# Score and maximum matmuls of two softmax attentions reading 64 and 62 rows of a half array in place of 50 and 48

## The reference

```
x = x + L0_xattn(_layernorm(x), ctx)      # softmax attention, 16 heads of 16
x = x + L0_ffn(_layernorm(x))             # top 2 of 8 experts
x = x + L1_xattn(_layernorm(x), ctx, ctx) # autocorrelation by FFT, top 6 lags
x = x + L1_ffn(_layernorm(x))             # top 1 of 4 experts
x = x + L2_xattn(_layernorm(x), ctx, ctx) # sigmoid attention
x = x + L2_ffn(_layernorm(x))             # shared part and top 2 of 8
x = x + L3_xattn(_layernorm(x), ctx)      # softmax attention
x = x + L3_ffn(_layernorm(x))             # top 1 of 16 scale and bias
```

## Time and profile before

| | us |
|---|---|
| runs, median (lowest, highest) | 2725.03 (2724.96, 2748.5) |
| the profiled execution | 2749.48 |
| its span, first to last instruction | 2747.7 |
| around the span (the difference) | 1.8 |
| TensorE / VectorE / ScalarE / GpSimd busy | 2600.0 / 1634.8 / 1573.2 / 326.9 |
| mean granted TensorE clock | 0.942 |

### The profile page before, as it was taken

One profiled execution on the slowest core, in us unless ns is written; L12 is line 12 of the kernel. 1 busy time (PEld: TensorE's weight loads), 2 busy tenths in 40 slices (PEclk: granted clock), 3 DMA queues, 4 the chain that ended last, 5 costly groups with the idle time before them and its releaser, 6 DMA issues.

```text
span 2747.7 us, 46488 instructions
## 1 busy us (share of the span) xinstructions
PE 2600.0 (95%) x18464; PEld 1281.6 (47%) x18464; DVE 1634.8 (59%) x2983; ACT 1573.2 (57%) x2691; POOL 326.9 (12%) x280
## 2 busy tenths in 40 slices
PE   7999999999899779999899999989999999999987
PEld 3334344333377657776233333268633343434433
DVE  6877788778387664442112221057587788878844
ACT  1777777776701112111687978932247777777763
POOL 2010100100003311121010010012201001010001
PEclk7899999998999889999999999989969899999988
DMA  5433334322210001001844646210043342334300
GB/s 120 72 37 38 61 43 67 45 29 25 73 29 16 1 16 54 1 1 36 123 49 73 72 64 75 52 51 1 14 59 60 37 73 36 38 61 48 38 1 31
DMA packets 68636, 125.13 MB, mean 46 GB/s; under 512 B 20979, under 2 KB 45630, under 8 KB 64966
## 3 DMA queue, kind: packets, MB, share of 16 engines
q1 hardware_dynamic: 67270, 119.73, 28.5%
q10 hardware_dynamic: 1152, 2.44, 0.4%
HBM read 41.59 MB, written 2.10 MB: 16 GB/s over the span
## 4 chain that ended last, share of the span: by engine, by line
PE 54%; DVE 4%; ACT 3%; issue 1%; SPq 1%; ACTq 0%; DMA 0%; POOL 0%; POOLq 0%; DVEq 0%
PE psum L202 24%; PE psum L748 13%; PE psum L213 9%; PE psum L2109 6%; ACT probs L816 2%; DVE mpart L938 2%; PE psum L308 1%; PE psum L2102 1%; SPq L1054 1%; DMA qst<-qp_lo 0%; SPq L1055 0%; PE psum L758 0%; ACTq L1054 0%; ACTq L1055 0%; DVE stats L335 0%
## 5 line engine op out<-in xcount | busy, mean ns | idle before, releaser
L816 ACT ACTIVATE probs<-psum 128x512 f32<-128x512 f32 (+3 forms) x2080 | 1266.4, 690 | 311.8 <-PE psum L202 304.0
L938 DVE TENSOR_REDUCE mpart<-psum 128x2 f32<-128x804 f32 x1024 | 972.6, 990 | 265.6 <-PE psum L202 254.6
L748 PE MATMUL psum<-probs,vt 128*17 128x512 f32 (+1 forms) x4992 | 674.1, 619 | 3.6 <-ACT probs L816 2.9
L202 PE MATMUL psum<-qst,kst 50*128 50x512 f32 (+3 forms) x2496 | 624.6, 450 | 18.8 <-ACT probs L816 7.7
L202 PE MATMUL psum<-kst,qst 48*128 48x402 f32 x2048 | 490.1, 426 | 22.4 <-DVE mpart L938 19.6
L202 PEld LDWEIGHTS psum<-qst,kst 50*128 50x128 f32 (+3 forms) x2496 | 294.7, 188 | 393.4 <-issue 212.5
L202 PEld LDWEIGHTS psum<-kst,qst 48*128 48x128 f32 x2048 | 240.5, 200 | 314.4 <-DVE mpart L938 174.6
L748 PEld LDWEIGHTS psum<-probs,vt 128*17 128x17 f32 (+1 forms) x4992 | 92.9, 96 | 218.9 <-issue 181.5
L213 PE MATMUL psum<-wv,ctxT 128*32 128x256 f32 (+1 forms) x2448 | 172.8, 402 | 0.8 <-DVE kp_lo L919 0.8
L213 PE MATMUL psum<-ctxT,wk 128*32 128x512 f32 (+1 forms) x1536 | 147.8, 510 | 11.8 <-DMA ctxT<-in_ctxT 9.4
L2154 ACT ACTIVATE inner<-psum 128x512 f32<-128x512 f32 x32 | 19.1, 597 | 211.8 <-PE psum L2109 211.8
(11 more groups left out here) (340 smaller groups left out, 2638.9 us busy)
## 6 DMA issues: line engine op xcount, KB each, us to landing
kst<-kp_hi SPq DMA_DIRECT2D x144, 200.1 KB, 5.8
ctxT<-in_ctxT SPq DMA_DIRECT2D x36, 512.0 KB, 5.2
kst<-kp_lo SPq DMA_DIRECT2D x72, 200.1 KB, 5.4
qst<-qp_hi SPq DMA_DIRECT2D x144, 64.0 KB, 4.5
kst<-kp_hi SPq DMA_DIRECT2D x84, 100.1 KB, 2.9
qst<-qp_lo SPq DMA_DIRECT2D x72, 64.0 KB, 5.1
kst<-kp_lo SPq DMA_DIRECT2D x42, 100.1 KB, 3.0
stage<-in_L_ffn_W SPq DMA_DIRECT2D x16, 256.0 KB, 4.3
```

Source lines behind the costliest of these rows:

```text
L202: last = e.matmul(dst, lhsT, rhs, start=i == 0, stop=i == len(pairs) - 1)
L748: t = e.matmul(c.bank(self.acc)[32 * h:32 * h + VW, :], self.vt[0:kn, kc, self.head(g, h), :], p[0:kn, h % self.wide, :], start=kc == 0, s ...
L816: e.activation(self.probs[n % slots][0:kn, :, :], c.psum[0:kn, k:k + self.wide, :], ACT.Exp if softmax else ACT.Sigmoid, scale=DH ** -0.5) ...
L938: e.tensor_reduce(self.mpart[:, :, p * (SEQ // P) + qt, i], c.psum[:, k:k + 2, 0:MAX_WIDTH], AX.X, ALU.max).then_inc(c.drained(k), 1)
```

## The change

The stack is 64 rows in each half. The three blocks stay in rows 0 to 47. The two rows of the maximum move from 48 and 49 to 62 and 63. The score matmuls contract all 64 rows, the maximum matmuls the first 62, so that they don't meet the rows of the maximum. The rows between are ones in `kst` and have to be zero in `qst`; GpSimd therefore fills each `qst` buffer with 0.0 before it fills the `kst` buffer with 1.0, and the loads of units 0 to 2 wait for both. The constants `STACK` and `MAX_AT` are used by the softmax attentions alone.

```
-STACK = PART_ROWS + MAX_ROWS
+STACK = 64
+MAX_AT = STACK - MAX_ROWS
...
                 for j in range(2):
-                    at = slice(64 * j, 64 * j + PART_ROWS)
+                    at = slice(64 * j, 64 * j + MAX_AT)
                     t = mm(e, c.bank(k + j)[:, 0:MAX_WIDTH], [(self.qst[u % 3][at, p, qt * P:(qt + 1) * P],
                                                                self.kst[u % 3][at, p, keys])])
...
         if softmax:
-            e.memset(self.kst[0].bitcast(F32)[:, :, :], 1.0).then_inc(c.sem("ones0"), 1)
+            self.clear(e, 0)
...
             if kind == "ones":
-                e.memset(self.kst[step[2]].bitcast(F32)[:, :, :], 1.0).then_inc(c.sem(f"ones{step[2]}"), 1)
+                self.clear(e, step[2])
...
+    def clear(self, e, u):
+
+        made = self.c.sem(f"ones{u}")
+        e.memset(self.qst[u].bitcast(F32)[:, :, :], 0.0).then_inc(made, 1)
+        e.memset(self.kst[u].bitcast(F32)[:, :, :], 1.0).then_inc(made, 1)
+
...
-            e.wait_ge(self.c.sem(f"ones{u}"), (0, 6).index(self.f) + 1)
+            e.wait_ge(self.c.sem(f"ones{u}"), 2 * (0, 6).index(self.f) + 2)
...
-                        row, of = 64 * j + PART_ROWS + i, 4 * GROUP * i + 2 * GROUP * j
+                        row, of = 64 * j + MAX_AT + i, 4 * GROUP * i + 2 * GROUP * j
```

## The result

| | before | changed |
|---|---|---|
| runs, median (lowest, highest), us | 2729.59 (2717.75, 2748.5) | 2699.24 (2695.17, 2702.41) |
| ratio to before, 95% interval | | 0.9859 (0.9825 to 0.9893) |
| profiled execution / span, us | 2749.48 / 2747.7 | 2698.66 / 2696.8 |
| mean granted clock | 0.942 | 0.966 |

By the ratio the changed kernel is 1.4% faster, with an interval of 1.1 to 1.8%. The two medians differ by 30.4 us, which is 1.1%; the profiled executions differ by 50.8 us, and that is the most favourable pair, as the profiled execution of before took longer than all six runs of its median. The forecast was 33 and 44.8. The runs of the changed kernel also lie closer together: 7 us from lowest to highest, where the kernel before has 31.

A forecast was written before the change was run, and what follows sets the result against it. TensorE was taken to bound the softmax units, slowed by clock falls; terms summed to 44.8 us, so 2749.5 became 2704.7 us profiled, less 12.2 to the median: 2692.5 us, range 2678 to 2730.

The forecast's parts named there:

- The forecast's case, that rows earn the clock: Softmax units: clock grant follows rows that work, so added rows remove falls; 2680 to 2705 us, likeliest 2692, chance 0.55.
- Rival 1: Softmax units: added rows earn nothing, falls stay; 2725 us, or up to 2748; chance 0.27.
- Rival 3: Every softmax unit: a fuller array falls more often; 2778 us if low time doubles; chance 0.07.
- Rival 2: Softmax units: rows earn half, as maxima stop at 62 rows; 22.4 us gained, 2708 us; chance 0.11.
- 31.9 + 4.0: Units 1 to 14, both softmax phases: 31.9 us back from six low units, 4.0 from three short falls.
- A low microsecond: Softmax units: each us at 1.2 GHz loses 0.37 us, from 31.9 us lost in 85.5 low ones.
- Units 0: First units of both softmax phases, low clock carried over from the prelude: half of at most 9.1 us back, 4.6.
- Added rows, fills, wait, moved DMAs: Costs of the change: taken as 0; range 0 to 4 us for rows, 0 to 5 for fills disturbing VectorE.
- the last unit of phase 6: 23.4 us low, at most 8.7 us back; half counted, 4.3, as part of its fall comes with real gaps.
- half of the 24.5 us between them: Profiled execution to median: half the gap put in other phases' falls, which stay, so 12.2 us off 2704.7, giving 2692.5.
- all in the softmax units: Bound of that step: all 24.5 us lie in falls the change removes anyway, so the median is 2705 us.
- the signs: Softmax units 3, 7, 11 take 40 to 41 us, unit 14 some 36, at 1.00; 64-row matmul minimum 386 to 388 ns.

The follow-up runs named there:

- the two phases of one execution: Changed kernel with phase 6 back at 50 and 48 rows, so 64 and 62 in phase 0 alone, fills kept: 2721.43 us, 0.9952 of before.
- the filler: Changed kernel plus one extra 128-row, 256-column matmul behind each maximum step of unit 0 in both preludes: 2715.62 us, 0.9913 of before.

## Why the prediction was right

*The cause.* The forecast's case, that rows earn the clock, held against all three rivals. The matmuls are still halves of the array, so it isn't their being halves. Rival 1 (nothing) fails with the change itself. That it is the rows and nothing beside them is shown by the fills alone, by the two phases of one execution, and by the kernel with maxima at 40, which has neither fills nor moved rows and differs the other way; the rows' contents don't matter either. Rival 3 (more rows cost clock) has the wrong sign: 8 rows less on the maxima added 48 us of low time in phase 0. Rival 2 (maxima at 62 rows would spoil half) fails too: 3.4 us low remain, and even maxima at 48 leave just a quarter. The low units of before were busy 45.0 of 45.1 us. By that, what the Trainium skill says in "TensorE: Matmul & The Clock Gate", section "What's actually happening", that the gate follows how busy TensorE has been, isn't enough here. In what measure the rows count (rows alone, or rows times columns) is open.

*The terms, against the profiled executions.* For units 1 to 14 I had 31.9 + 4.0 = 35.9; measured 37.4. A low microsecond is worth 37.4 / 92.2 = 0.41, not 0.37, mostly because unit 3 at full clock takes 39.6 us and I had compared it with a 40.5 us unit. Units 0: 4.6 and 4.8, with some luck: unit 0 of phase 0 was 14.8 to 15.1 us low in three executions with 50 and 48 rows and 7.6 in the changed kernel, but also only 6.6 with maxima at 40. Added rows, fills, wait, moved DMAs: 0, and 0 seen. The mis-sized term is the last unit of phase 6: half of 8.7, 4.3, on the ground that part of its fall comes with real gaps; it gave 8.3. But that unit is a loose one: it was 13.4 to 23.9 us low in eight executions with scores of 50 rows, 3.4 to 13.7 in four with 64 and 62, 17.1 with 56, and 23.9 with the scores alone at 64, though it holds no maxima. So its 8.3 us can't be put down to its own rows; what led up to it counts too, and I leave open how.

*From the profiled execution to the median.* This step failed. I put half of the 24.5 us between them into the other phases. The second profile of before shows that of 16.2 us less, 13.8 lie in phase 6's own units (671.9 to 658.1 us), which the change cures anyway. By the bound "all in the softmax units" I had 2705 where 2692 was stated; with the last unit's term right it would have been 2701, and 2699.2 was measured. The changed kernel's profiled execution and median are within 1 us of each other (2698.7 and 2699.2), so what made the longest runs of before went with the change, and with it the wider spread. That 30.4 us in the medians came so near the 33 is partly luck: the profiled gain was 6.0 us more than the sum of terms, and the 12.2 us put down to other phases were not there; the two errors have opposite signs.

*The range and the sign.* 2678 to 2730 held. Whether it is over 1% faster, to which I gave 0.42, is close: the ratio says 1.4%, the medians 1.1%, and 2699.2 is 1.4 us over the 2697.8 at which I drew the line. The doubt was mainly about rows or halves, which no row of before could settle. Of the signs, units 7 and 11 took 40.5 us, unit 3 a little less than the 40 to 41 set (39.6), and unit 14 took 35.9 and 35.3, the first with 3.4 us low; the fastest 64-row matmul took 383 ns, under the 386 to 388 set.

## What to carry to other kernels

Where TensorE is busy without a gap and its granted clock still falls, look at how much of the array the matmuls of that stretch fill. Filling a half-array contraction up with zero rows cost no time in the matmul here and one fill a buffer, and gave back 1.1 to 1.4%. Look for it in stretches that TensorE bounds; where VectorE bounded a prelude, a higher clock bought with extra work didn't pay. Be careful with a contraction of 32 rows among ones of 50: it cost 7 us a unit here, for a reason that wasn't isolated. And take more than one profile, as which units fall can differ between executions of one kernel.

## What the runs showed that was not expected

- More rows earn more clock, with falling return: low time of phase 0's units 1 to 14 was 102.4 us with maxima at 40 rows, 54.6 with scores at 50 and maxima at 48 (three executions alike), 17.1 at 56 and 54, and 0 to 3.4 at 64 and 62 (five executions without the filler).
- What the added rows of `qst` hold doesn't matter: zeros and ones gave the same 3.4 us.
- Maxima of 32 rows among scores of 50 made a unit at full clock 50.3 us for 43.1.
- The falls of phase 0 repeated in three executions of 50 and 48 rows to 0.1 us in sum, while phase 6, in five, gave 41.0, 41.0, 17.1, 17.1 and 34.1.
- Twice the clock, bought with filler matmuls, brought nothing in a prelude that VectorE bounds: the filler's records, 431 ns in the mean, stand in the order between the maxima, and TensorE, busy 26.96 of 27.5 us, became the bound.
